# Graph products kept with features on partitions: the norm as a per-partition affine, the slope as a maximum, and transposes back to rows

## The reference, cut to what matters

```
h = x @ W
deg = segment_sum(1, dst) + 1 (self loop);  dinv = rsqrt(deg)
out = segment_sum(h[src] * dinv[src] * dinv[dst], dst) + conv_bias
mu = out.mean();  xc = out - mu;  std = sqrt((xc * xc).mean())      # over all nodes and features
y = xc / (std + EPS) * ln_weight + ln_bias
gnn = where(y >= 0, y, prelu_a * y)
x = x + gnn + attention
x = x + experts(layernorm(x))        # top 2 of 8 experts for each row
```

## Time and profile before

| | us |
|---|---|
| median of 3 runs (lowest, highest) | 1373.95 (1372.21, 1378.43) |
| span of the profiled execution | 1377.2 |
| first products | 790 to 837 |
| chain to mu and std | 837 to 845 |
| loop of the second products | 845 to 925 |
| norm, routing, sorting | 925 to 974 |
| experts | 974 to 1377 |

### The profile page before, as it was taken

One profiled execution on the slowest core, in us unless ns is written; L12 is line 12 of the kernel. 1 busy time (PEld: TensorE's weight loads), 2 busy tenths in 40 slices (PEclk: granted clock), 3 DMA queues, 4 the chain that ended last, 5 costly groups with the idle time before them and its releaser, 6 DMA issues. The chain is left out here.

```text
span 1377.2 us, 30864 instructions
## 1 busy us (share of the span) xinstructions
PE 1245.3 (90%) x8354; PEld 1106.3 (80%) x8355; DVE 962.4 (70%) x2966; ACT 539.3 (39%) x1443; POOL 854.3 (62%) x836
## 2 busy tenths in 40 slices
PE   4997688999899999999898797985799999999998
PEld 4984687887788888887787686873699999999997
DVE  8998787887888777778693288998444444444444
ACT  7707301222333333333311101446455555555553
POOL 1294677777777777777777202431376666666665
PEclk9999899999999999999999898995799999999999
DMA  7005333335666666789898400449244444444443
GB/s 245 0 0 183 111 106 103 107 105 172 194 194 199 198 191 202 207 246 277 260 288 261 144 1 16 138 155 318 64 77 66 68 71 69 72 69 70 71 69 42
DMA packets 138148, 186.89 MB, mean 136 GB/s; under 512 B 21438, under 2 KB 116468, under 8 KB 137916
## 3 DMA queue, kind: packets, MB, share of 16 engines
q0 software_dynamic: 43440, 90.29, 28.7%
q1 hardware_dynamic: 94604, 95.40, 21.8%
HBM read 153.16 MB, written 33.41 MB: 135 GB/s over the span
## 5 line engine op out<-in xcount | busy, mean ns | idle before, releaser
L740 POOL DMA_INDIRECT RG<-table,srci x484 | 477.3, 986 | 153.0 <-issue 149.4
L757 PEld LDWEIGHTS ps<-S_t,RG 128*128 128x128 f32 x1936 | 259.2, 196 | 39.0 <-DMA RG<-table,srci 28.6
L757 PE MATMUL ps<-S_t,RG 128*128 128x96 f32 x1936 | 266.4, 278 | 21.6 <-DMA RG<-table,srci 21.1
L780 PE MATMUL ps<-zrow,R 128*128 128x256 f32 (+1 forms) x784 | 221.1, 389 | 15.2 <-DMA zrow<-table 8.7
L2010 POOL DMA_INDIRECT out<-R,S_t x105 | 166.3, 1584 | 99.5 <-DVE R L1980 55.8
L1893 PE MATMUL ps<-R,RG 128*128 128x128 f32 x1680 | 207.3, 277 | 0.0
L1893 PEld LDWEIGHTS ps<-R,RG 128*128 128x128 f32 x1680 | 198.3, 194 | 0.4 <-issue 0.4
L1903 PE MATMUL ps<-R 128*128 x840 | 198.5, 379 | 0.0
L1014 DVE TENSOR_TENSOR R<-R,ps 128x245 f32 (+4 forms) x300 | 142.1, 474 | 73.7 <-PE ps L768 52.5
L1926 ACT ACTIVATE R<-ps,RG 128x128 f32<-128x128 f32 x420 | 120.0, 368 | 175.8 <-PE ps L1893 175.8
L1976 DVE TENSOR_TENSOR R<-ps,R 128x256 f32<-128x256 f32 x105 | 44.6, 425 | 200.8 <-PE ps L1903 200.8
(11 more groups left out here) (360 smaller groups left out, 1989.9 us busy)
## 6 DMA issues: line engine op xcount, KB each, us to landing
zrow<-table SPq DMA_DIRECT2D x384, 128.0 KB
RG<-table,srci POOLq DMA_INDIRECT x484, 3.3
ntable<-R SPq DMA_DIRECT2D x12, 516.0 KB
table<-RG SPq DMA_DIRECT2D x12, 512.0 KB, 2.9
out<-R SPq DMA_DIRECT2D x12, 512.0 KB, 3.2
R<-in_x SPq DMA_DIRECT2D x6, 896.0 KB, 11.7
R<-in_w SPq DMA_DIRECT2D x8, 514.0 KB, 6.4
slot<-in_x SPq DMA_DIRECT2D x32, 128.0 KB
```

Of the source, the lines that this page charges most:

```text
L740: nc.gpsimd.indirect_dma_start(out=grows[:, s, :], out_offset=None, in_=table, in_offset=bass.IndirectOffsetOnAxis(ap=srci[:, ND + q, c:c ...
L757: last = nc.tensor.matmul(window(q % 2)[:, h, :], grows[:, s, h * P:(h + 1) * P], S_t[:, q % 2, c, :], start=c == 0, stop=c == GC - 1)
L780: nc.tensor.matmul(psD[:, 0:D], adj[b % 2][0:n, j, :], zrow[0:n, i % ZR, :], start=j == 0, stop=j == T - 1).then_inc(z_used, 1)
```

## The change

The products are made once. W is the stationary operand and 500 nodes of `acc` move, so the result has features on partitions; DVE multiplies it by `dall`, which holds `dinv` of every node on every partition, straight back into `acc` (bias left out), and takes statistics of pieces of 250. Mean and deviation follow from these and the bias per feature. The norm is then one affine per feature, with a scale and a bias per partition: ACT applies it in place to slabs of four tiles (512 columns), DVE bends the slab with max(prelu_a * y, y), PE turns each tile back to rows by two transposes, and DVE adds it to the residual from PSUM. If prelu_a is over 1, a sign `side` turns the maximum into a minimum. The second products, the negative part on ACT and the residual sum on POOL go.

For `dall`, `dinv` (128 x 49) is turned by PE and copied by DVE during the aggregation, stored to HBM, and loaded to all partitions once the first half of `R1` is free (the seventh of the eight dense blocks turned). The bias, weight and shift of the norm come as two numbers per partition each. Row statistics of x are joined behind the loop, for all tiles at once, by seven instructions instead of one per tile.

```diff
+PIECE = 250; NPIECE = N // PIECE; SPAN = 2 * PIECE; NSPAN = -(-N // SPAN)
+SLAB = 4 * P; NSLAB = -(-T // 4)
...
+        dall = R1[:, 0:N]
...
@@ aggregation, SP
+                    if q == B1 + 6:
+                        sp.wait_ge(dr_ok, 1)
+                        sp.dma_start(dflat.rearrange("(t p) -> t p", p=P), ksl[0:T, 0, :]).then_inc(dr_out, 16)
+                sp.wait_ge(dr_out, 16)
+                sp.wait_ge(blk_t, NDB - 1)
+                sp.dma_start(dall, dflat[0:N].unsqueeze(0).to_broadcast([P, N])).then_inc(da_in, 16)
                 sp.wait_ge(pe_done, GQ - 2)
                 sp.dma_start(gw, a_gw.rearrange("(k p) n -> p k n", p=P)).then_inc(late, 16)
-                sp.dma_start(cbias, a_cb.unsqueeze(0).to_broadcast([P, D])).then_inc(late, 16)
-                sp.dma_start(lnw, a_lnw.unsqueeze(0).to_broadcast([P, D])).then_inc(late, 16)
-                sp.wait_ge(pe_done, GQ - 1)
-                sp.dma_start(lnb, a_lnb.unsqueeze(0).to_broadcast([P, D])).then_inc(late, 16)
+                for dest, source in ((cbf, a_cb), (lnwf, a_lnw), (lnbf, a_lnb)):
+                    sp.dma_start(dest[:, :], source.rearrange("(k p) -> p k", p=P), ...).then_inc(late, 16)
                 sp.wait_ge(late, 16 * 4)
+                sp.wait_ge(da_in, 16)
@@ aggregation, PE and DVE
+                    if q == B1 + 1 and r == 0:
+                        pe.wait_ge(qt_ok, T)
+                        nc.tensor.transpose(psT[0:T, :], dinv[:, :], ident[:, :]).then_inc(mid_pe, 1)
+                    if q == B1 + 1 and r == 2:
+                        v.wait_ge(mid_pe, 6)
+                        nc.vector.tensor_copy(ksl[0:T, 0, :], psT[0:T, :]).then_inc(dr_ok, 1)
@@ PE
+                def features(i):
+                    j, f = i // KC, i % KC
+                    if i >= 6:
+                        pe.wait_ge(u_ok, i - 5)
+                    lo, hi = j * SPAN, min(j * SPAN + SPAN, N)
                     for k in range(KC):
-                        last = nc.tensor.matmul(ps[t % 4][:, 0:D], acc[:, k, t * P:(t + 1) * P], gw[:, k, :],
+                        last = nc.tensor.matmul(ps[i % 6][:, 0:hi - lo], gw[:, k, f * P:(f + 1) * P], acc[:, k, lo:hi],
                                                 start=k == 0, stop=k == KC - 1)
                     last.then_inc(pr_ok, 1)
...
-                def scaled(t):
+                def back(t):
+                    pe.wait_ge(pr_in, KC * (t // 4 + 1))
                     if t >= 2:
-                        pe.wait_ge(v_ok, t - 1)
+                        pe.wait_ge(x_ok, t - 1)
                     for k in range(KC):
-                        last = nc.tensor.matmul(psW[t % 2][:, 0:D], acc[:, k, t * P:(t + 1) * P], wx[:, k, :], ...)
+                        last = nc.tensor.transpose(psW[t % 2][:, k * P:(k + 1) * P], acc[:, k, t * P:(t + 1) * P],
+                                                   ident[:, :])
                     last.then_inc(px_ok, 1)
...
-                for s in range(T + 5): scaled(s), flip(s - 4), logits(s - 5)
+                for s in range(T + 3): back(s), flip(s - 2), logits(s - 3)
@@ ACT
-                def negative(t): ...
+                def affine(c):
+                    lo, hi = c * SLAB, min(c * SLAB + SLAB, NP)
+                    for k in range(KC):
+                        act.activation(acc[:, k, lo:hi], acc[:, k, lo:hi], ACT.Identity, scale=aw[:, k:k + 1],
+                                       bias=bw[:, k:k + 1]).then_inc(af_ok, 1)
...
+                act.wait_ge(fn_ok, 1)
+                for c in range(2):
+                    affine(c)
+                for t in range(T):
+                    if t % 4 == 0 and t // 4 + 2 < NSLAB:
+                        affine(t // 4 + 2)
+                    flipped(t)
@@ POOL
-                for t in range(T):
-                    residual(t)
@@ DVE
-                def rows(t): ...; def row_stats(t): ...
+                def scaled(j):
+                    lo, hi = j * SPAN, min(j * SPAN + SPAN, N)
+                    v.wait_ge(pr_ok, KC * j + KC)
+                    for f in range(KC):
+                        nc.vector.tensor_tensor(acc[:, f, lo:hi], ps[(KC * j + f) % 6][:, 0:hi - lo], dall[:, lo:hi],
+                                                ALU.mult).then_inc(u_ok, 1)
+                def feature_stats(j):
+                    v.wait_ge(u_ok, KC * j + KC)
+                    for f in range(KC):
+                        for i in range(2 * j, min(2 * j + 2, NPIECE)):
+                            last = nc.vector.bn_stats(fstats[:, f, i, :], acc[:, f, i * PIECE:(i + 1) * PIECE])
+                    return last
...
-                ch.done(nc.vector.tensor_scalar(aw, lnw, d2, None, ALU.mult))
-                ch.done(nc.vector.tensor_tensor(wx, gw, aw.unsqueeze(1).to_broadcast([P, KC, D]), ALU.mult))
-                v.sem_inc(wx_ok, 1)
+                ch.done(nc.vector.tensor_tensor(d2, d2, side, ALU.mult))
+                ch.done(nc.vector.tensor_scalar(aw, lnwf[:, :], d2, None, ALU.mult))
+                ch.done(nc.vector.scalar_tensor_tensor(bw, cbf[:, :], mu, aw, ALU.subtract, ALU.mult))
+                ch.done(nc.vector.scalar_tensor_tensor(bw, lnbf[:, :], side, bw, ALU.mult, ALU.add))
+                v.sem_inc(fn_ok, 1)
...
-                def shifted(t): ...
+                def bent(c):
+                    lo, hi = c * SLAB, min(c * SLAB + SLAB, NP)
+                    for k in range(KC):
+                        v.wait_ge(af_ok, KC * c + k + 1)
+                        nc.vector.scalar_tensor_tensor(acc[:, k, lo:hi], acc[:, k, lo:hi], pre[:, 0:1], acc[:, k, lo:hi],
+                                                       ALU.mult, ALU.max).then_inc(pr_in, 1)
                 def finish(t):
-                    v.wait_ge(ng_ok, t + 1)
-                    v.wait_ge(xa_ok, t + 1)
-                    nc.vector.scalar_tensor_tensor(halved(o_all[:, t, :]), halved(minus[:, t % 4, :]), a1, o_tile(t), ...)
+                    v.wait_ge(px_ok, t + 1)
+                    nc.vector.scalar_tensor_tensor(halved(o_all[:, t, :]), halved(psW[t % 2][:, 0:D]), side, o_tile(t),
                                                    ALU.mult, ALU.add).then_inc(x_ok, 1)
...
-                for s in range(T + 4): shifted(s), x_stats(s - 3), x_stats_joined(s - 4), finish(s - 2)
+                bent(0)
+                for s in range(T + 1):
+                    if s % 4 == 0 and s // 4 + 1 < NSLAB:
+                        bent(s // 4 + 1)
+                    finish(s), x_stats(s - 1)
+                v.wait_ge(st_ok, T)
+                (7 instructions of 128x49: mean and variance of each row from the two halves of bn_stats)
```

More of the change, by code:

```diff
@@ L56 @@
 W1ROW = KC * HID + HC
+PIECE = 250
+NPIECE = N // PIECE
+SPAN = 2 * PIECE
+NSPAN = -(-N // SPAN)
+assert NPIECE * PIECE == N
+SLAB = 4 * P
+NSLAB = -(-T // 4)
 def build(nc, a_x, a_src, a_dst, a_gw, a_cb, a_lnw, a_lnb, a_pre, a_wqkv, a_mk, a_mv, a_wout, a_bout,
@@ L131, in build @@
         pre = sb("pre", [P, 1])
+        cbf, lnwf, lnbf = (RG[:, 16 * D + KC * k:16 * D + KC * (k + 1)] for k in range(3))
         brr = sb("brr", [P, NX])
@@ L1396, in build @@
             psF = [ps[2], ps[3]]
[L1397 removed]
+            turned = zrow[:, 0:2, :]
             psL, psR, psC8, psI = ps[4], ps[5], ps[6], ps[7]
@@ L1457, in rows @@
                                                 start=k == 0, stop=k == KC - 1)
                     last.then_inc(pr_ok, 1)
-                for t in range(4):
-                    rows(t)
+                for i in range(4):
+                    features(i)
                 pe.wait_ge(g_ok, 2)
                 for k in range(KC):
-                    nc.tensor.matmul(ps[5][:, 0:NX], betas[:, k, :], wr[:, k, :], start=k == 0, stop=k == KC - 1)
+                    nc.tensor.matmul(ps[6][:, 0:NX], betas[:, k, :], wr[:, k, :], start=k == 0, stop=k == KC - 1)
@@ L1465, in _ @@
                 for k in range(KC):
-                    last = nc.tensor.matmul(ps[6][:, 0:NX], ones[:, :], wrg[:, k, :], start=k == 0, stop=k == KC - 1)
+                    last = nc.tensor.matmul(ps[7][:, 0:NX], ones[:, :], wrg[:, k, :], start=k == 0, stop=k == KC - 1)
                 last.then_inc(g_ps, 1)
-                for t in range(4, T):
-                    rows(t)
+                for i in range(4, KC * NSPAN):
+                    features(i)
                 for n in range(2):
@@ L1471, in _ @@
                     pe.wait_ge(part, n + 1)
[L1472 to L1476, removed]
-                def scaled(t):
+                    for k in range(KC):
+                        last = nc.tensor.matmul(ps[7][:, n:n + 1], ones[:, :], tot2[:, k:k + 1], start=k == 0,
+                                                stop=k == KC - 1)
@@ L1500, in logits @@
                     last.then_inc(l_ps, 1)
-                for s in range(T + 5):
+                for s in range(T + 3):
                     if s < T:
```

(26 more changed lines are left out.)

115 lines of the change are left out of this document (38 added, 77 removed).

## The result

The changed kernel takes 1381.4 us (median of 10 runs, 1376.15 to 1385.87) beside 1374.37 us (10 runs, 1371.16 to 1381.38): ratio 1.0046, 95% interval 1.0027 to 1.0065. It is slower by about half a per cent, where 1.1% faster was forecast. The profiled execution took 1381.24 us, 1.84 more than its span.

A forecast was written before the change was run, and what follows sets the result against it. PE was taken to bound the first products and DVE the loop. Terms 0.3 + 1.5 + 0.3 - 0.6 - 2.2 - 16.9 + 1.5 + 1.05 = -15.05 us took 1373.95 to 1359 us, range 1353 to 1368.

The forecast's parts named there:

- cold start: Loop entry: PE starts transposes at half clock, three tiles cost 0.5 us more each: +1.5 us, bounds 0 and 3.5.
- first rival: Loop: transposes and 8-column products don't raise the clock, PE sets the pace, about 1393 us; decides from 1.46 per tile; chance 0.05.
- Rows of `dinv`: Aggregation: one PE transpose, a DVE copy and a 25 KB store are added: +0.3 us, bounds 0 and 1.
- `dall`: Before the first products: its 3.2 MB load lands late, +1.5 us, bounds 0 and +14; rival eating the gain, 1371.7, chance 0.07.
- End of the first products: Behind the last product: two multiplications and two statistics instead of one and one, +0.3 us, bounds -0.5 and +1.
- Chain: Small steps between first products and lead-in: one goes, two wide ones become four small: -0.6 us, bounds -0.9 and 0.
- Lead-in: Chain to first `finish`: ACT makes and DVE bends two slabs, 3.7 us against 5.9: -2.2 us, bounds -3 and 0.
- Loop: Second products' loop: DVE sets 1.15 us per tile, 55.2 us against 72.1: -16.9 us, bounds -19.8 and -11.6.
- coupling: Loop: two PSUM buffers make PE wait during bends, some 0.25 us in four tiles, so 1.15 us per tile over 1.09.
- After the loop: Behind the loop: seven instructions of 128x49 replace the last two joins, +1.05 us, bounds 0.7 and 1.5.
- The contention of `finish`: Loop: rival that `finish` stays at 0.74 us without POOL, giving back 11 us, 1370 us; chance 0.05.
- The stores: Behind the loop: rival that 2.2 MB of transfers remain for the next stage, giving back 8 us, 1367 us; chance 0.07.

The follow-up runs named there:

- experiment 1: Changed kernel with PE's idle time from the last first product to the loop filled by 46 wide bf16 products: 1352.73 us, ratio 0.9831 to the kernel before.
- experiment 3: Changed kernel with every tile turned back by ordinary fp32 products with the unit matrix instead of transposes: 1359.95 us, ratio 0.9877 to the kernel before.
- experiment 5: Changed kernel with six bf16 products of 512 columns added between the chain and the first turn back: 1354.78 us, ratio 0.9846 to the kernel before.
- experiment 6: Changed kernel with only the first four tiles turned back by product instead of transpose, nothing filled: 1354.12 us, ratio 0.9836 to the kernel before.
- experiment 2: Changed kernel with one bf16 product of 512 columns added per tile in the loop: 1358.25 us, ratio 0.9866 to the kernel before.
- experiment 8: Changed kernel without the load of `dall`, multiplying by ones, so degree scaling is missing from the result: 1377.4 us, one run.
- experiment 9: Changed kernel with wide products filling PE ahead of the loop, and first-product spans of 250 instead of 500: 1352.91 us, ratio 0.9833 to the kernel before.
- experiment 10: Changed kernel filled ahead of the loop, spans of 250, with 13 instead of 22 fillers after the last first product: 1349.58 us, ratio 0.9813 to the kernel before.
- experiment 11: Changed kernel with the first four tiles turned back by product and first-product spans of 250, nothing filled: 1353.98 us, ratio 0.9831 to the kernel before.

## Why the prediction was wrong, step by step

**The step that failed** is the cold start: "Three tiles at 0.5 more: +1.5". It took for granted that the loop's own work would raise the clock after three tiles. It never did: 0.50 for all of the 75 us. This was the first rival, given 0.05, and it came about at its place (the loop, PE setting the pace) and beyond its point of decision (1.60 us per tile against 1.46). Only its price was too high: from the first `finish` to the last (848.97 to 923.15) a tile takes 1.545 us on average, the first few being shorter, and with that it gives 1359 - 1.5 + 48 x (1.545 - 1.15) = 1376.5 us, not 1393; the measurement is 1381.4.

Why was it given 0.05? Because of the early stage, whose transposes went from 421 to 273 ns. That reading was right, and the window's granted clock of 1.00 is not: the trace's first record of the granted clock stands at 115.93 us, and a window ahead of it reads 1.00 for want of a record. The weight loads of that stretch show the rise at the same place:

```profile
115.23 0.29 PEld L464 LDWEIGHTS ps<-ident,RG 128*128 128x128 f32 x2 [0.20 <-ACT RG L330]
115.73 0.27 PEld L464 LDWEIGHTS ps<-ident,RG 128*128 128x128 f32 x2 [0.20 <-ACT RG L330]
116.22 0.20 PEld L464 LDWEIGHTS ps<-ident,RG 128*128 128x128 f32 x2 [0.22 <-ACT RG L330]
```

They are pairs behind an idle PEld. Such a pair takes 0.29 us in the changed kernel's loop, at a recorded 0.50, and 0.20 in experiment 1's, at a recorded 1.00:

```profile
849.56 0.29 PEld L1505 LDWEIGHTS ps<-ident,R 128*128 128x128 f32 x2 [1.16 <-DVE R L1694]
```

```profile
844.27 0.20 PEld L1515 LDWEIGHTS ps<-ident,R 128*128 128x128 f32 x2 [1.45 <-DVE R L1704]
```

In all 13 profiles the first record stands between 115.1 and 118.3 us, and in each the weight loads become shorter within half a microsecond of it. Ahead of the stage, bf16 products of 49 columns had kept PE busy for 55 us without bringing a record, and ended 3.28 us before its first transpose. So transposes, with nothing else on PE from 111.8 us on, did raise the clock there. What failed is the step from that stage to the loop: the stage has no products of 8 columns, and in the loop they take 0.71 of a tile's 1.60 us. That they are what keeps the clock low fits: in experiments 3, 5 and 6 the clock rose ahead of the first of them (by 0.70, 0.03 and 0.16 us), and only in experiment 2, with a wide product per tile, behind it (0.28). It is not shown, for no run leaves them out of the loop.

The Trainium skill's page "TensorE: Matmul & The Clock Gate", Part 4, says that the full clock does not engage for transpose mode. The prediction set that aside by the early stage, whose transposes did engage it (115.93 us). The loop entered at 0.50 came out as that sentence would have it (75 us at 0.50), but doesn't consist of transposes alone; entered at 1.00 it kept 1.00 for 49 us (experiment 1).

**The other steps**, from the table of stages:

- *Rows of `dinv`, +0.3*: too small to be told; the aggregation's end varies by 10 us.
- *`dall`, +1.5*: +0.35 in the two profiles, about +1.0 over all of them (experiment 8): somewhat less than forecast, and far from the bound of 14. Its load was issued at 769.45, 2 us sooner than assumed, and took 14.4 us beside the tails.
- *End of the first products, +0.3*: +2.28, mis-sized. Behind the last product come not two statistics but six (2.01 us): DVE's order is multiply span j+1, then statistics of span j, so the four of the span ahead are still waiting. Experiments 9 to 11 gave back 1.4.
- *Chain, -0.6*: -0.13. The small steps went as counted; the two sums of PE take 1.02 and 1.01 us at 0.50, and at 1.00 the chain takes 6.54.
- *Lead-in, -2.2*: -2.15, right, with 3.73 us against 3.7.
- *Loop, -16.9*: +2.33. At 1.00 it is -23.97 (filled) or -22.66 (four by product), more than forecast. A tile inside it takes DVE 0.71 us and a quarter of the 1.32 of two bends, from start to start: 1.04 against 1.09. Two of the 13 slabs are bent ahead of the first `finish`, which leaves 1.00 per tile, and the 0.06 of coupling isn't there: DVE has no gap. PE's 1.09 was too high: 8.58 us of 10 in the filled loop.
- *After the loop, +1.05*: +1.38.

The remaining rivals didn't come about. The contention of `finish` went with POOL's work (742 to 483 ns), as argued. The stores didn't bind behind the loop even when it took 49 us: 203 GB/s in it, and 3.75 us to the first norm.

## What to carry to other kernels

When a change takes the wide products out of a loop and leaves transposes and narrow products, ask at which clock the loop is *entered*, and read the granted clock of the stretch ahead of it. An earlier stage is evidence only if it runs the same mix: here a stage of transposes alone raised the clock, and a loop of transposes and 8-column products did not. Check a granted clock against the durations of like instructions at a known level; where they disagree, look whether the trace has a record there at all. If the loop is entered at the lower level, a few ordinary products at its beginning may be worth more than all that was saved: here 4 tiles turned by product instead of by transpose made 1381 us into 1354. And when spans are pipelined by one, count the work of the span ahead as well behind the last product.

## What the runs showed of the hardware

- A loop of transposes of 128x128 and products of 8 columns, PE busy 10.00 of 10 us, left the granted clock at 0.50 for 75 us. The same loop kept it at 1.00 for 49 us with PE busy 8.58 of 10 (878 to 888 us). Transposes alone, two to a tile, raised it in the early stage of the kernel before (115.93 us) and then kept 1.00 (a window of it, all engines):

```profile
124.00:136.00 12.00, 10.50 (x49) 4.82 (x48) 12.00 (x38) 11.35 (x24) 4.83 (x12) 1.00 0.78 263
```
- From 0.50 it rose with ordinary fp32 products of 128 columns (experiments 3 and 6), with one bf16 product of 512 columns per tile (2), and some 3 us after six of these had ended, with transposes on PE (5).
- What in the loop's mix keeps the clock from rising, and what holds it once it is up, the transposes or the 8-column products, was not tried.
- Halving the clock cost this loop's PE work a factor of about 1.9 (0.86 us per tile as 8.58 of 10 at one tile per us, against 1.60).
